# A sort stage of five operations with the weights going between two buffers, and one stream of sorts over three walks, in a graph-and-feed-forward kernel

## The reference, cut to what matters

```python
def gnn(x, weight, row, col, vals):           # x is layernormed
    h = jnp.einsum('nf,ef->ne', x, weight)
    msgs = vals[:, None] * h[col]
    return jax.ops.segment_sum(msgs, row, num_segments=8192)
x = x + gnn(_layernorm(x), L0_gnn_weight, src, dst, edge_weight)
x = x + ffn(_layernorm(x)[None], L0_ffn_W, L0_ffn_b)[0]
```

## Time and profile before

| | us |
|---|---|
| median of 3 runs | 1778.88 (1778.59 to 1779.0) |
| the profiled execution | 1777.97 |
| its span, first to last instruction | 1776.2 |
| TensorE busy (4076 instructions) | 1633.4 |
| VectorE busy (4540) | 1173.2 |
| ScalarE busy (1354) | 604.1 |
| GpSimd busy (1114) | 1065.1 |
| first build of a walk, start | 278.69 |

### The profile page before, as it was taken

How to read it: one execution, slowest core, us unless ns; L and a number is a source line. 1 busy time by engine, 2 the same in 40 slices (tenths; PEclk the granted TensorE clock), 3 DMA queues, 4 the chain that set the end, 5 groups by cost and what they waited for, 6 DMA issues and landing times.

```text
span 1776.2 us, 29342 instructions
## 1 busy us (share of the span) xinstructions
PE 1633.4 (92%) x4076; PEld 651.5 (37%) x4077; DVE 1173.2 (66%) x4540; ACT 604.1 (34%) x1354; POOL 1065.1 (60%) x1114
## 2 busy tenths in 40 slices
PE   7999997999999999999999999999999999995995
PEld 4455542433333423333333233333343333332442
DVE  7666656777777787778777877878743333335465
ACT  7777732222222222222222122222244444443341
POOL 1000005777777777777667677776777777775930
PEclk9999998999999999999999999999999999998798
DMA  7334215777777777766667676766677777772334
GB/s 256 119 133 136 91 68 167 212 209 207 209 206 207 209 207 204 203 198 196 191 191 202 189 202 192 203 193 188 192 209 210 209 209 210 210 209 64 131 111 140
DMA packets 121766, 323.92 MB, mean 182 GB/s; under 512 B 20434, under 2 KB 39154, under 8 KB 121586
## 3 DMA queue, kind: packets, MB, share of 16 engines
q0 software_dynamic: 81920, 268.50, 53.2%
q1 hardware_dynamic: 39666, 53.48, 8.9%
HBM read 288.35 MB, written 33.55 MB: 181 GB/s over the span
## 4 chain that ended last, share of the span: by engine, by line
PE 55%; DVE 16%; DMA 9%; issue 8%; POOL 7%; DVEq 3%; ACT 1%; SPq 1%; ACTq 0%; POOLq 0%
PE psum L1201 34%; PE psum L1109 12%; DMA region<-h_rows,region 9%; POOL region L519 7%; DVE region L918 5%; PE psum L1280 4%; DVEq L918 2%; DVE region L827 2%; DVE region L817 2%; PE psum L1098 2%; DVE region L821 1%; DVE region L829 1%; DVE region L831 1%; DVE region L823 1%; PE psum L1248 1%
## 5 line engine op out<-in xcount | busy, mean ns | idle before, releaser
L519 POOL DMA_INDIRECT region<-h_rows,region x1024 | 984.8, 962 | 615.9 <-DMA h_rows<-region 268.8
L1201 PE MATMUL psum<-region 128*128 x2552 | 1237.3, 617 | 84.2 <-DVE region L918 44.8
L1201 PEld LDWEIGHTS psum<-region 128*128 128x128 f32 x2552 | 433.3, 189 | 849.9 <-issue 845.7
L918 DVE SCALAR_TENSOR_TENSOR region<-region 128x128 f32 (+1 forms) x1276 | 450.5, 353 | 437.8 <-PE psum L1201 290.7
L679 ACT ACTIVATE x<-psum 128x512 f32<-128x512 f32 x192 | 114.6, 597 | 784.8 <-PE psum L1201 784.8
L1109 PE MATMUL psum<-region 128*128 128x512 f32 x512 | 230.2, 593 | 0.8 <-ACT region L581 0.8
L831 DVE COPY_PREDICATED region<-region 128x128 f32<-128x128 int32 x452 | 159.0, 352 | 0.0
L827 DVE COPY_PREDICATED region<-region 128x128 f32<-128x128 int32 x452 | 158.1, 350 | 0.0
L662 ACT ACTIVATE psum<-x 128x512 f32<-128x512 f32 x256 | 153.7, 601 | 8.0
L817 DVE TENSOR_TENSOR region<-region 128x128 int32<-128x128 f32 x452 | 130.4, 289 | 23.1 <-ACT region L608 21.5
L829 DVE TENSOR_TENSOR region<-region 128x128 f32<-128x128 f32 x452 | 136.4, 302 | 0.0
(11 more groups left out here) (150 smaller groups left out, 637.9 us busy)
## 6 DMA issues: line engine op xcount, KB each, us to landing
x<-in_x SPq DMA_DIRECT2D x16, 1024.0 KB, 6.1
h_rows<-region SPq DMA_DIRECT2D x64, 256.0 KB, 2.0
region<-h_rows,region POOLq DMA_INDIRECT x1024, 3.7
out<-x SPq DMA_DIRECT2D x4, 2816.0 KB, 10.8
out<-x SPq DMA_DIRECT2D x8, 640.0 KB, 3.4
region<-in_L_gnn_weight SPq DMA_DIRECT2D x1, 1024.0 KB, 5.5
region<-in_src SPq DMA_DIRECT2D x4, 128.0 KB, 2.5
region<-in_dst SPq DMA_DIRECT2D x4, 128.0 KB, 2.4
```

The costliest lines, as they stand in the source:

```text
L519: pool.indirect_dma_start(gathered[:, (c + 1) % RING, :], None, h_dram, bass.IndirectOffsetOnAxis(ap=dst_i[g][:, i:i + 1], axis=0),).then_ ...
L918: dve.scalar_tensor_tensor(spread[:, slot % SR, :], iota_n[:, bass.ds((tile - (g * T + 1)) * P, P)], src_f[g][:, bass.ds(chunk - (g * NC + ...
L1201: pe.matmul(banks[:, bass.ds(pe.snap(tile_wanted) % AGG, 1), :].rearrange("p t f -> p (t f)"), spread[:, slot % SR, :], gathered[:, bass.d ...
```

## The change

- A level has five operations. The keys slot writes is_gt, a copy of all 256 weights into the other buffer, and the min. The weights slot writes the max and one predicated copy of 256 elements, in which the mask is read twice and the weights in exchanged halves. Keys and weights both go to and fro between two buffers, the second of which, `other_weights`, lies where `low_kept` was (128 words per partition larger).
- In parts 1 to 3 the turned weights are not copied out of PSUM: the first level after a turn reads them there. The turned keys are still copied.
- "pack" copies the weights once into the other buffer.
- The planner assumes 0.65 us each for keys and weights (0.6 and 0.85 before). With that `HEAD` goes from 40 to 59 slots, and each turn of part 0 stands one tile earlier.
- `slots_with_steps` makes one stream of the sorts of parts 1 to 3 over the steps of three walks, with no free steps at the end of walks 0 and 1: 1105 slots over 945 steps, 1.095 steps for a full slot (before 1.078 in walk 0, 0.957 in walks 1 and 2). Weights and turned slots have a share of 0.9.
- `RING` goes from 11 to 10.

```diff
-    RING = 11
+    RING = 10
...
-    def slots_with_steps(g):
...
+    def slots_with_steps():
+
+        left = [(g, slot) for g in range(1, PARTS) for slot in SORT_SLOTS[HEAD if g == 1 else 0:]]
+
+        def share(what):
+            return {"keys": 1.0, "weights": 0.9, "turned": 0.9, "flip": 0.4, "rest": 0.5}.get(what, 0.7)
+
+        shares = [share(what) for _, (what, _, _) in left]
+        room = ((PARTS - 1) * NS - LAST_STEPS) / sum(shares)
+        found, at = [0] * (PARTS * NS), 0.0
+        for (g, _), of_one in zip(left, shares):
+            step = int(at * room)
+            assert step < g * NS - LAST_STEPS
+            found[step] += 1
+            at += of_one
         return found
...
-        SORT_STEPS = {"pack": 2, "flip": 1, "keys": 3, "weights": 3}
+        SORT_STEPS = {"pack": 3, "flip": 1, "keys": 3, "weights": 2}
+        BY_SCALAR = (TURNS, HEAD_TURNS) + (0,) * (PARTS - 2)
...
-                        dve.tensor_copy(kept, low_w).then_inc(s_sort[g], 1)
+                        dve.tensor_copy(weights[1 - now], weights_now).then_inc(s_sort[g], 1)
...
                     elif what == "weights":
                         dve.wait_ge(s_sort[g], done - 1)
-                        dve.copy_predicated(low_w, swap, high_w).then_inc(s_sort[g], 1)
+                        dve.tensor_tensor(to_high, low, high, ALU.max).then_inc(s_sort[g], 1)
                         dve.wait_ge(s_sort[g], done)
-                        dve.tensor_tensor(to_high, low, high, ALU.max).then_inc(s_sort[g], 1)
-                        dve.wait_ge(s_sort[g], done + 1)
-                        dve.copy_predicated(high_w, swap, kept).then_inc(s_sort[g], 1)
-                        done += 3
+                        dve.copy_predicated(both(weights[1 - now], j),
+                                            swap.unsqueeze(2).to_broadcast(both(weights_now, j).shape),
+                                            both(weights_now, j)[:, :, ::-1, :]).then_inc(s_sort[g], 1)
+                        done += 2
...
-                        if turns > (TURNS, HEAD_TURNS, 0, 0)[g]:
+                        if turns <= BY_SCALAR[g]:
+                            dve.wait_ge(s_key_in[g], turns)
+                        else:
+                            weights_now = turned_weights
                             dve.wait_ge(s_turn_k[g], turns)
-                            dve.tensor_copy(keys[now], turned_keys).then_inc(s_key_in[g], 1)
-                            dve.wait_ge(s_turn_w[g], turns)
-                            dve.tensor_copy(weight[g], turned_weights).then_inc(s_wgt_in[g], 1)
-                        dve.wait_ge(s_key_in[g], turns)
+                            dve.tensor_copy(keys_now, turned_keys).then_inc(s_key_in[g], 1)
+                            dve.wait_ge(s_key_in[g], turns)
```

More of the change, by code:

```diff
@@ L101, in gnn_ffn @@
     assert sum(what == "turn" for what, _, _ in SORT_SLOTS) == TURNS
+    assert sum(what == "weights" for what, _, _ in SORT_SLOTS) % 2 == 1
     def plan():
-        vector_times = {"pack": 6.0, "flip": 0.3, "keys": 0.6, "weights": 0.85, "turned": 1.9, "maxima": 2.5,
+        vector_times = {"pack": 6.0, "flip": 0.3, "keys": 0.65, "weights": 0.65, "turned": 1.9, "maxima": 2.5,
                         "counts": 2.0, "rows": 2.0, "index": 0.4, "source": 0.8}
@@ L135, in gnn_ffn @@
     HEAD_TURNS = sum(what == "turn" for what, _, _ in SORT_SLOTS[:HEAD])
-    def slots_with_steps(g):
-        left = SORT_SLOTS[HEAD if g == 0 else 0:] if g + 1 < PARTS else []
-        share = {"keys": 1.0, "weights": 1.0, "turned": 1.2, "flip": 0.4, "rest": 0.5}
-        room = (NS - LAST_STEPS) / max(1.0, sum(share.get(what, 0.7) for what, _, _ in left))
-        found, at = [0] * NS, 0.0
-        for what, _, _ in left:
-            found[int(at * room)] += 1
-            at += share.get(what, 0.7)
+    def slots_with_steps():
[10 more added lines that the diff above has]
+            at += of_one
         return found
@@ L204, in gnn_ffn @@
         keys = [carve(NC), carve(NC)]
-        rest = carve(NC + NC // 2)
+        rest = carve(2 * NC)
         swaps = [rest[:, i * NC // 2:(i + 1) * NC // 2].bitcast(I32) for i in range(2)]
-        low_kept = rest[:, NC:NC + NC // 2]
-        below = low_kept
+        other_weights = rest[:, NC:2 * NC]
+        below = other_weights[:, 0:NC // P * T]
         over = rest[0:T, 0:NSP]
@@ L768, in sort_edges, with both @@
                 done = turns = now = half = 0
+                weights = weights_of(g)
+                keys_now, weights_now = keys[0], weights[0]
+                def both(a, j):
+                    return a.rearrange("p (b s d) -> p b s d", s=2, d=1 << (j if j < 7 else j - 7))
                 def pairs(a, j):
-                    v = a.rearrange("p (b s d) -> p b s d", s=2, d=1 << (j if j < 7 else j - 7))
-                    return v[:, :, 0, :], v[:, :, 1, :]
+                    return both(a, j)[:, :, 0, :], both(a, j)[:, :, 1, :]
                 def single(a, j):
@@ L925, in _ @@
                 dve.wait_ge(s_hst[u], 16 * (T // 4))
-            for g in range(PARTS):
-                following = second if g == 0 else sort_edges(g + 1)
-                for i, slots in enumerate(slots_with_steps(g)):
-                    build(g, i)
-                    for _ in range(slots):
-                        next(following)
-                    if g == 0 and i == SR:
-                        for cleared in (all_fwT, all_fw_in, bias.rearrange("p h l -> p (h l)"), fw_out[:, :]):
-                            dve.memset(cleared, 0.0).then_inc(s_fz, 1)
+            following = chain(second, *[sort_edges(g) for g in range(2, PARTS)])
+            for at, slots in enumerate(slots_with_steps()):
+                build(*divmod(at, NS))
+                for _ in range(slots):
+                    next(following)
+                if at == SR:
+                    for cleared in (all_fwT, all_fw_in, bias.rearrange("p h l -> p (h l)"), fw_out[:, :]):
+                        dve.memset(cleared, 0.0).then_inc(s_fz, 1)
             go, = counters(dve, "dve_live")
@@ L1115, in turn_edges @@
                 pe.wait_ge(s_sort[g], steps - 1)
-                if turn or g:
-                    pe.wait_ge(s_key_in[g if turn else g - 1], turn if turn else TURNS)
+                if 0 < turn <= BY_SCALAR[g]:
+                    pe.wait_ge(s_key_in[g], turn)
                 for b in range(NC // P):
@@ L1204, in add_step @@
                           start=False, stop=True, skip_group_check=True).then_inc(s_done, 1)
-            for g in range(PARTS):
-                following = islice(SORT_SLOTS, HEAD if g == 0 else 0, None)
-                for i, slots in enumerate(slots_with_steps(g)):
-                    add_step(g, i)
-                    for what, _, _ in islice(following, slots):
-                        of_sort(g + 1, what)
+            following = chain.from_iterable(((g, what) for what, _, _ in SORT_SLOTS[HEAD if g == 1 else 0:])
+                                            for g in range(1, PARTS))
+            for at, slots in enumerate(slots_with_steps()):
+                add_step(*divmod(at, NS))
+                for of_part, what in islice(following, slots):
+                    of_sort(of_part, what)
             assert turned == [TURNS] * PARTS
```

25 lines of the change are left out of this document (15 added, 10 removed).

## The result

The changed kernel takes 1771.43 us (median of 9 runs, 1768.55 to 1778.58) against 1779.0 (1778.11 to 1788.14) of the kernel before beside it: ratio 0.9949, 95% interval 0.9929 to 0.9969. It is faster, but by 7.6 us where 32 were forecast, and outside the range of 1740 to 1764.

A forecast was written before the change was run, and what follows sets the result against it. GpSimd's gathers were taken to bound the kernel, with VectorE slower in walks 1 and 2: 1778.0 - 36 (those waits) + 4 (longer gathers) = 1746, with 0.9 to the median 1747 us; range 1740 to 1756, widened to 1764.

The forecast's parts named there:

- What bounds the kernel: The four walks: GpSimd's gathers pace walks 0 and 3; VectorE slows walks 1 and 2, losing 36 us.
- Weights slot: VectorE's weights step: max of 128 and one predicated copy of 256 take W = 0.81 us, bounds 0.81 and 1.12.
- W: Time of a VectorE step with a weights slot, taken as 0.81 us; today's mean 1.12.
- near end: The lower bound of W, 0.81 us, taken because predicated copies go at the pace of min and max.
- Keys slot: VectorE's keys step with a copy of 256: stays at 1.06 us, cost zero, between 0 and +0.13 us.
- turned slot: VectorE's slot after a turn, without the 0.34 us weights copy: taken at zero, at best -15 us of VectorE.
- the cover: Time in the keys step before the next build, which hides the longer copy: 1.01 us of work under 1.06.
- One stream: Sorts spread over three walks: VectorE needs 876 us, GpSimd 963, so all walks run at GpSimd's pace, -36 us.
- Ten slots: Gather slots cut from 11 to 10: zero, between 0 and +4 us.
- Head stage: Before the walks, part 0's turns move one tile earlier: zero, between -2 and +3 us.
- Gathers under longer copies: GpSimd's gathers lengthened by 313 copies of twice the elements: +4 us, between 0 and +9.
- Rival 3: Gathers are held for the whole VectorE copy: +28 us instead of +4, 1771 us; chance 0.06.

The follow-up runs named there:

- e11: The changed kernel, with the is_gt waiting until the build before it has finished: 1751.29 us, ratio 0.9856.
- e3: The kernel before (six operations, eleven slots, old head) with only the new single stream of sorts: 1772.09 us, ratio 0.9951.
- e4: The changed kernel with the old spreading of sort slots by walk, so without the single stream: 1763.38 us, ratio 0.9892.
- e7: The kernel before with its keys-slot copy taking all 256 weights and with ten slots, all else old: 1780.47 us, ratio 1.0000.
- e1: The changed kernel with the plain weights copy made a max of the weights with themselves, except after a turn: 1822.31 us, ratio 1.0221.
- e18: The changed kernel with the is_gt waiting for the build and the predicated copy split into two of 128: 1741.88 us, ratio 0.9800.
- e2: The changed kernel with the copy of 256 weights issued as two of 128, except after a turn: 1810.73 us, ratio 1.0152.
- e5: The changed kernel with the keys slot in the order is_gt, min, copy: 1797.72 us, ratio 1.0112.
- e15: The changed kernel with the predicated copy split into two of 128, no waits: 1991.13 us, ratio 1.0034, in a comparison where every kernel took some 200 us more.
- e9: The changed kernel with the weights copy moved from the keys slot to the head of the weights slot: 1799.17 us, ratio 1.0096.
- e14: The changed kernel, is_gt waiting for build, copy for is_gt, predicated copy split in two: 2005.7 us, ratio 1.0145, every kernel there some 200 us slower.

## Why the prediction was wrong, step by step

- **What bounds the kernel**: right. GpSimd's pace, and VectorE behind it in walks 1 and 2; the idle time fell by the 36.0 us that were read as the loss.
- **Weights slot**: right, W = 0.84 for 0.81, close to the near end. A reversed read and a repeated mask go at the pace of a plain predicated copy, 0.33 us for 256 elements. The working noted that the register work moves ahead, so that the build follows at once, and counted this as pure gain. That same closed gap is what lengthens the gathers (e11).
- **Keys slot, turned slot**: right, 1.09 for 1.06 us, within the cover. VectorE waits 103.8 us for the turned keys, which costs nothing, since no gather waits.
- **One stream**: its forecast held only together with the stage. The claim that the sum closes even with the old W within 9 us isn't borne out: e3 has 29.8 us of waits left. It also sorts 9.5 levels more in the walks, for which its expectation allowed, and that gave 5 to 15. And the term of 36 us doesn't need the stream: e4 has the waits gone without it.
- **Ten slots**: right at zero (e7). **Head stage**: right at zero, the first gather starts at 277.4 us, before at 278.0. The first turn of part 0 stands one tile earlier, at 50.43 us (before 54.34, forecast 50.5).
- **Gathers under longer copies**: this step failed. It took +4 us with bounds 0 to +9, and 28 were measured; its own sign of being wrong, gathers over 985 ns on average, came up (989 on the page). It sized the loss per copy, from the means of walks 0 and 3, and scaled it with the copy's elements; the runs show that copies of 256 alone cost nothing (e7: 963 ns) and that the loss depends on whether VectorE's run over the build is broken by a gap, ahead of the build (e7) or behind it (e11). The bound was no bound, because the rows it came from are of a kernel that has that gap: none of its 63 gathers issued in the first 0.2 us of an is_gt stands behind a run without one.
- **Rival 3** gave 1771, the time measured, and its +28 us is the size measured. Its mechanism, a gather held for the length of one copy, isn't it: without the plain copy the loss more than doubles (e1: 1054 - 964 = 90 ns for 37), and with one as long in the old stage it vanishes (e7). That the price fits, 313 x 0.09, is chance.
- Sum by the profiled executions: 1778.0 - 0.6 (start) - 36.0 + 28.2 = 1769.6, measured 1770.8. In e18: 1778.0 + 1.9 - 36.0 - 768 x 0.0057 = 1739.5, measured 1740.1. The five operations with a wait added (e11) come to 1751.3, 4 us above the forecast of 1747; only with the predicated copy in two, six operations again, does the time fall below it.

**What stays open.** The runs show that the long holds (gathers above 1.3 us) are there in every kernel in which the weights slot, the build and the keys slot run without a gap (after, e1, e2, e4, e5, e15) or the keys slot, the build and the weights slot do (e9), and in none in which a wait opens a gap of 0.11 us or more ahead of the is_gt, the copy or the min, or the old weights slot leaves one ahead of the build (before, e3, e7). They don't show by what GpSimd and VectorE exclude each other, why a run inside one slot (e7) is harmless where one over the build isn't, why a hold ends with the slot's last operation even where the build follows at once (e5), nor why some gathers in a run without a gap aren't held. Why the split helps beyond e11 (959 for 976 ns) is shown only as far as the holds behind the predicated copy of 256 are gone with it.

## What to carry to other kernels

Where GpSimd's indirect gathers set the pace, VectorE's work isn't free just because VectorE has time left. Read the single gathers, not only their mean: look for those above the common duration and for what VectorE did around their start. Fewer VectorE instructions that follow one another more closely can cost the pace-setter most of what they save, here 28 of 36 us; a wait that opens a gap of 0.1 us once per group of operations can give it back. A loss that is measured in one pattern of operations bounds nothing in another.

## What the runs showed of the hardware that was not expected

- An indirect gather of 128 rows takes 0.95 us undisturbed. Issued with the is_gt of a run of VectorE operations without a gap (predicated copy, build, is_gt, copy, min) it mostly takes 1.31 to 1.51 us, issued with the build up to 1.56, and up to 1.77 with a sixth operation in the run (e2).
- A held gather ends 0.82 us behind the end of the keys slot's last operation: all 46 of the kernel after (min), and 103 of 109 in e5 (copy), in 94 of which the build follows without a gap.
- The holds repeat: 1.56 + 0.30 us of a held gather equals the period of VectorE's keys and weights steps, 1.86 us (e1), so that one hold puts the next gather at the same place.
- A wait that opens 0.11 us in each keys slot of VectorE (e11) takes 19 us off the kernel; with the predicated copy split, 30.7 us (e18, both by the profiled executions). The same split without the wait leaves the mean gather at 1025 ns (e15, on the chip where e14 has 966).
- A plain copy of 256 elements lasts 0.29 us where one of 128 lasts 0.22, and from start to start 0.20 where one of 128 takes 0.13; the max of 256 with two inputs lasts 0.42 (e1), and a predicated copy of 256 takes 0.33 from start to start.
